# The opening of a two-stage graph network kernel, put in another order on all five engines

## The reference, cut to what matters

```python
h = jnp.maximum(_layernorm(x), 0.0)
x = x + _L0_gnn_ref(h, adj, W, a)      # masked attention, only the 16 largest weights of a row are kept, elu
h = jnp.maximum(_layernorm(x), 0.0)
x = x + _L1_gnn_ref(h, adj, ...)       # three layers
# one layer of L1:
scores = leaky(x @ w_i + (x @ w_j).T + b), -inf outside of (adj or the diagonal)
h  = layernorm(x + softmax(scores) @ x) * g1 + beta1
ff = gelu(h @ W1 + b1) @ W2 + b2       # 256 -> 1024 -> 256
x  = layernorm(h + ff) * g2 + beta2
```

## Time and profile before

| | |
|---|---|
| median of three runs | 2843.44 us (2842.48 to 2846.93) |
| span of the profiled execution, first to last instruction | 2840.5 us |
| PE busy | 2719.1 us, 96% of the span |
| PE weight load busy | 2449.2 us, 86% |
| ACT busy | 2326.9 us, 82% |
| DVE busy | 2293.8 us, 81% |
| POOL busy | 2080.0 us, 73% |
| mean granted clock of PE | 0.979 |

### The profile page before, as it was taken

The page is one execution under the profiler, slowest core; times in us unless marked ns, Lnnn a source line. Parts: engine busy times, 40 slices in busy tenths (PEclk is TensorE's granted clock), DMA queues, the critical chain, the costliest instruction groups (busy, mean ns, idle before and its releaser), DMA issues.

```text
span 2840.5 us, 55392 instructions
## 1 busy us (share of the span) xinstructions
PE 2719.1 (96%) x17764; PEld 2449.2 (86%) x17764; DVE 2293.8 (81%) x7766; ACT 2326.9 (82%) x4806; POOL 2080.0 (73%) x2217
## 2 busy tenths in 40 slices
...
DMA packets 96322, 88.63 MB, mean 31 GB/s; under 512 B 9120, under 2 KB 94368, under 8 KB 96032
## 3 DMA queue, kind: packets, MB, share of 16 engines
...
## 4 chain that ended last, share of the span: by engine, by line
PE 80%; POOL 5%; issue 5%; DVE 4%; ACT 3%; DMA 2%; POOLq 0%; SPq 0%; ACTq 0%; DVEq 0%
PE ps_ff L3065 11%; PE ps_mm L3042 11%; PE ps_mm L3044 11%; PE ps_mm L3043 10%; PE ps_ff L3066 10%; PE ps_ff L3067 10%; PE ps_ag L3100 5%; PE ps_ht L3112 3%; PE ps L3164 2%; DMA out<-H 2%; POOL a_lo L506 2%; PE ps_s L3088 1%; PE ps_s L3078 1%; PE ps L3177 1%; PE ps L3178 1%
## 5 line engine op out<-in xcount | busy, mean ns | idle before, releaser
L3065 PE MATMUL ps_ff<-w_hi,a_hi 128*128 128x256 f32 x3072 | 892.0, 290 | 10.1 <-POOL a_lo L506 5.3
L506 POOL TENSOR_TENSOR a_lo<-A,a_hi 128x512 fp32r<-128x512 f32 x384 | 524.3, 1366 | 486.7 <-ACT a_hi L1077 486.4
L3066 PE MATMUL ps_ff<-w_lo,a_hi 128*128 128x256 f32 x3072 | 855.6, 279 | 0.0
L3067 PE MATMUL ps_ff<-w_hi,a_lo 128*128 128x256 f32 x3072 | 855.0, 278 | 0.0
L1069 ACT ACTIVATE A<-ps_mm,b_col 128x512 f32<-128x512 f32 x768 | 517.3, 685 | 251.7 <-PE ps_ff L3067 147.8
L3042 PE MATMUL ps_mm<-ht_hi,w_hi 128*128 128x512 f32 x1536 | 627.0, 408 | 3.7 <-DVE ht_lo L2327 2.8
L3065 PEld LDWEIGHTS ps_ff<-w_hi,a_hi 128*128 128x128 f32 x3072 | 578.2, 188 | 45.7 <-issue 11.7
L3044 PE MATMUL ps_mm<-ht_lo,w_hi 128*128 128x512 f32 x1536 | 606.5, 395 | 0.0
L3043 PE MATMUL ps_mm<-ht_hi,w_lo 128*128 128x512 f32 x1536 | 604.6, 394 | 0.0
L3066 PEld LDWEIGHTS ps_ff<-w_lo,a_hi 128*128 128x128 f32 x3072 | 579.0, 188 | 12.5
L3067 PEld LDWEIGHTS ps_ff<-w_hi,a_lo 128*128 128x128 f32 x3072 | 579.2, 189 | 0.0
...
## 6 DMA issues: line engine op xcount, KB each, us to landing
...
X<-in_L_gnn_W SPq DMA_DIRECT2D x3, 1024.0 KB, 5.2
H<-in_L_gnn_W SPq DMA_DIRECT2D x3, 1024.0 KB, 7.1
```

Of the source, the lines that this page charges most:

```text
L506: pool.tensor_tensor(a_lo[:, at], A[:, at], a_hi[:, at].bitcast(F32), ALU.subtract).then_inc(s["a_lo_gpsimd"], 1)
L3065: pe.matmul(out_g, a_hi[:, at, cols], w2_hi[:, l, m], start=first, stop=False, skip_group_check=True)
L3066: pe.matmul(out_g, a_hi[:, at, cols], w2_lo[:, l, m], start=False, stop=False, skip_group_check=True)
L3067: last = pe.matmul(out_g, a_lo[:, at, cols], w2_hi[:, l, m], start=False, stop=final, skip_group_check=True)
```

## The change

All five opening() lists keep the same calls, in another order. iteration(i), closing() and every function that the lists call are as before. SP, ACT, DVE and PE have 56, 347, 309 and 330 calls, POOL 245.

In the new lists the loads of x(0), a0, W0 and of two adjacencies come ahead of W1(0) and W2(0). DVE begins with x_moments(0), ACT with x0_norm(0). The splits of the weights and bias_cols, bias_rows, w1_bias stand at other places: w1_low(1) ahead of z_max(1) and scores_mask(0,0), w1_low(2) ahead of y1_sum(1,0,0), w2_low(1) among the a_low of (0,0), w2_low(2) among those of (1,0), w1_bias(2) behind z_mix(1,0). masks(1), masks(2) and masks(3) stand earlier. From the first mm1 on, the order of attention, stage 0 and products changes at many places. The diff, cut; the lists go on in this manner:

```diff
@@ -328,61 +328,61 @@
 sp.dma_start(mask_in[:, l].rearrange("p g m -> p (g m)"), mask_park[value(k)]).then_inc(s_mask[l], 16)
 
 def opening():
-load_w0()
-load_w1(0)
 load_x(0)
 load_a0()
+load_w0()
+load_adj(0)
+load_adj(1)
 load_cols()
+park_mask(0)
+load_w1(0)
+load_w2(0)
+load_adj(2)
+load_wij()
 load_x(1)
-load_adj(0)
-load_w2(0)
+load_w1(1)
+load_mask(0, 0)
+store_x1(0)
+load_w2(1)
 load_rows()
-load_adj(1)
-load_wij()
-load_w1(1)
-park_mask(0)
-load_w2(1)
+park_mask(1)
+load_x(2)
 load_w1(2)
-load_w2(2)
-park_mask(1)
-load_mask(0, 0)
-load_adj(2)
-load_x(2)
-store_x1(0)
-park_mask(2)
-load_mask(1, 0)
-load_mask(0, 1)
-store_x1(1)
 load_x(3)
 load_adj(3)
...
@@ -544,170 +544,173 @@
 r_coefs(0)
 h_coefs(0, 0)
 h_scale(0, 0, 0)
+x_coefs(2)
+a_low(0, 0, 0)
 h_scale(0, 0, 1)
-h_bias(0, 0, 0)
-a_low(0, 0, 0)
-h_bias(0, 0, 1)
-x_coefs(2)
 a_low(0, 0, 2)
 r_coefs(1)
 a_low(0, 0, 4)
+h_bias(0, 0, 0)
+h_bias(0, 0, 1)
 a_low(0, 0, 6)
 y_coefs(0, 0)
 y_scale(0, 0, 0)
+y_bias(0, 0, 0)
 y_scale(0, 0, 1)
-y_bias(0, 0, 0)
 y_bias(0, 0, 1)
 h_coefs(1, 0)
+h_scale(1, 0, 0)
+x_coefs(3)
+a_low(1, 0, 0)
+h_scale(1, 0, 1)
 h_coefs(0, 1)
-h_scale(1, 0, 0)
+a_low(1, 0, 2)
 h_bias(1, 0, 0)
-h_scale(1, 0, 1)
-a_low(1, 0, 0)
+r_coefs(2)
+a_low(1, 0, 4)
+h_scale(0, 1, 0)
 h_bias(1, 0, 1)
-a_low(1, 0, 2)
-r_coefs(2)
-h_scale(0, 1, 0)
-a_low(1, 0, 4)
-x_coefs(3)
+h_bias(0, 1, 0)
+h_scale(0, 1, 1)
+h_bias(0, 1, 1)
 a_low(1, 0, 6)
-h_scale(0, 1, 1)
 a_low(0, 1, 0)
-h_bias(0, 1, 0)
 y_coefs(1, 0)
 a_low(0, 1, 2)
+x_coefs(4)
 y_scale(1, 0, 0)
 y_scale(1, 0, 1)
+h_coefs(2, 0)
 y_bias(1, 0, 0)
 y_bias(1, 0, 1)
 a_low(0, 1, 4)
 a_low(0, 1, 6)
-h_bias(0, 1, 1)
-h_coefs(2, 0)
...
@@ -1204,352 +1204,352 @@
 act.activation(flat(el[:]), flat(x1[:, two]), ACT.Exp).then_inc(s["elu_exped"], 1)
 
 def opening():
+x0_norm(0)
+wa_copy()
 w0_high()
-w1_high(0)
-wa_copy()
-w2_high(0)
-x0_norm(0)
 z_leaky(0)
 z_exps(0)
-w1_high(1)
-w2_high(1)
+w2_high(0)
+w1_high(0)
 z_copy(0)
 mix_high(0, 0)
 elu_exp(0, 0)
 mix_high(0, 1)
+w1_high(1)
 elu_exp(0, 1)
 x0_norm(1)
-w2_high(2)
 r_norm(0)
-w1_high(2)
+z_leaky(1)
 leaky(0, 0)
+z_exps(1)
 exps(0, 0)
 p_copy(0, 0)
-z_leaky(1)
-z_exps(1)
+w2_high(1)
+z_copy(1)
+mix_high(1, 0)
 h_norm(0, 0)
-z_copy(1)
 ht_high(0, 0, 0)
-mix_high(1, 0)
+mix_high(1, 1)
+elu_exp(1, 0)
 ht_high(0, 0, 1)
+x0_norm(2)
 gelu(0, 0, 0)
-mix_high(1, 1)
+gelu(0, 0, 1)
 a_high(0, 0, 0)
-gelu(0, 0, 1)
 a_high(0, 0, 1)
+elu_exp(1, 1)
 gelu(0, 0, 2)
-elu_exp(1, 0)
 a_high(0, 0, 2)
-elu_exp(1, 1)
 gelu(0, 0, 3)
+z_leaky(2)
+gelu(0, 0, 4)
 a_high(0, 0, 3)
-gelu(0, 0, 4)
 a_high(0, 0, 4)
+r_norm(1)
 gelu(0, 0, 5)
+w1_high(2)
 a_high(0, 0, 5)
-r_norm(1)
 gelu(0, 0, 6)
 a_high(0, 0, 6)
 gelu(0, 0, 7)
 a_high(0, 0, 7)
 leaky(1, 0)
-x0_norm(2)
+exps(1, 0)
+z_exps(2)
+p_copy(1, 0)
 y_norm(0, 0)
-exps(1, 0)
-p_copy(1, 0)
-z_leaky(2)
+w2_high(2)
+z_copy(2)
+mix_high(2, 0)
+h_norm(1, 0)
 leaky(0, 1)
-z_exps(2)
+ht_high(1, 0, 0)
 exps(0, 1)
+ht_high(1, 0, 1)
+mix_high(2, 1)
 p_copy(0, 1)
-h_norm(1, 0)
...
+a_high(1, 1, 2)
+ht_high(0, 2, 0)
+z_leaky(4)
+gelu(1, 1, 3)
+y_norm(2, 0)
+ht_high(0, 2, 1)
+a_high(1, 1, 3)
 leaky(3, 0)
-gelu(1, 1, 0)
-a_high(1, 1, 0)
-gelu(1, 1, 1)
-a_high(1, 1, 1)
+gelu(1, 1, 4)
+a_high(1, 1, 4)
 exps(3, 0)
-gelu(1, 1, 2)
+gelu(1, 1, 5)
+gelu(1, 1, 6)
 p_copy(3, 0)
-gelu(1, 1, 3)
-a_high(1, 1, 2)
-a_high(1, 1, 3)
-y_norm(2, 0)
-h_norm(0, 2)
-z_leaky(4)
-gelu(1, 1, 4)
-ht_high(0, 2, 0)
-a_high(1, 1, 4)
-gelu(1, 1, 5)
 a_high(1, 1, 5)
-ht_high(0, 2, 1)
-gelu(1, 1, 6)
+z_exps(4)
+a_high(1, 1, 6)
 gelu(1, 1, 7)
-a_high(1, 1, 6)
+gelu(0, 2, 0)
 a_high(1, 1, 7)
 leaky(2, 1)
-gelu(0, 2, 0)
-z_exps(4)
 a_high(0, 2, 0)
+gelu(0, 2, 1)
 exps(2, 1)
-gelu(0, 2, 1)
+z_copy(4)
 a_high(0, 2, 1)
 gelu(0, 2, 2)
+mix_high(4, 0)
 a_high(0, 2, 2)
 p_copy(2, 1)
+h_norm(3, 0)
 y_norm(1, 1)
+ht_high(3, 0, 0)
 gelu(0, 2, 3)
+gelu(0, 2, 4)
 a_high(0, 2, 3)
-gelu(0, 2, 4)
 a_high(0, 2, 4)
+elu_exp(4, 0)
 gelu(0, 2, 5)
-z_copy(4)
+mix_high(4, 1)
+gelu(0, 2, 6)
 a_high(0, 2, 5)
-h_norm(3, 0)
-ht_high(3, 0, 0)
-mix_high(4, 0)
-gelu(0, 2, 6)
 a_high(0, 2, 6)
-leaky(1, 2)
+ht_high(3, 0, 1)
+h_norm(2, 1)
 gelu(0, 2, 7)
 a_high(0, 2, 7)
-ht_high(3, 0, 1)
-h_norm(2, 1)
+elu_exp(4, 1)
+ht_high(2, 1, 0)
+leaky(1, 2)
+gelu(3, 0, 0)
...
@@ -2354,315 +2354,315 @@
 moments("y", n, lambda g: H[:, l, g])
 
 def opening():
+x_moments(0)
 wa_sums()
-x_moments(0)
 masks(0)
+e0_scores(0)
 w0_low()
-w1_low(0)
-e0_scores(0)
-w2_low(0)
 z_mask(0)
 z_max(0)
+masks(1)
 z_topk(0)
-bias_cols(0)
 z_recip(0)
-w2_low(1)
+w1_low(0)
 mix_low(0, 0)
-w1_low(1)
+x_moments(1)
 z_out(0, 0)
+w2_low(0)
+mix_low(0, 1)
 elu(0, 0)
-mix_low(0, 1)
-x_moments(1)
-masks(1)
 z_out(0, 1)
 elu(0, 1)
 r_moments(0)
+e0_scores(1)
 node_scores(0, 0)
+z_mask(1)
+w1_low(1)
+z_max(1)
 scores_mask(0, 0)
 scores_max(0, 0)
-e0_scores(1)
-w1_low(2)
+z_topk(1)
 recip(0, 0)
+z_recip(1)
+bias_cols(0)
+bias_rows()
 y1_sum(0, 0, 0)
-z_mask(1)
-z_max(1)
+masks(2)
 y1_sum(0, 0, 1)
 y1_moments(0, 0)
-z_topk(1)
+mix_low(1, 0)
+x_moments(2)
+z_out(1, 0)
+ht_low(0, 0, 0)
 bias_cols(1)
-w2_low(2)
-ht_low(0, 0, 0)
+mix_low(1, 1)
+ht_low(0, 0, 1)
+elu(1, 0)
+z_out(1, 1)
 bias_cols(2)
-mix_low(1, 0)
-bias_rows()
-ht_low(0, 0, 1)
-z_recip(1)
-z_out(1, 0)
-masks(2)
-mix_low(1, 1)
-x_moments(2)
-z_out(1, 1)
+e0_scores(2)
 a_low(0, 0, 1)
-elu(1, 0)
 elu(1, 1)
 r_moments(1)
+w2_low(1)
 a_low(0, 0, 3)
+z_mask(2)
+z_max(2)
+node_scores(1, 0)
 a_low(0, 0, 5)
-node_scores(1, 0)
+masks(3)
 a_low(0, 0, 7)
 scores_mask(1, 0)
+scores_max(1, 0)
 y_sum(0, 0)
+recip(1, 0)
 y_moments(0, 0)
-e0_scores(2)
-scores_max(1, 0)
-recip(1, 0)
+w1_low(2)
+y1_sum(1, 0, 0)
+z_topk(2)
+y1_sum(1, 0, 1)
+y1_moments(1, 0)
 node_scores(0, 1)
-z_mask(2)
-y1_sum(1, 0, 0)
-z_max(2)
+mix_low(2, 0)
 scores_mask(0, 1)
 scores_max(0, 1)
-y1_sum(1, 0, 1)
-y1_moments(1, 0)
...
@@ -3182,335 +3182,335 @@
 
 def opening():
 turn_wa()
+turn_e0(0)
 w1_bias(0)
-turn_e0(0)
-w1_bias(1)
 turn_z(0)
 z_mix(0, 0)
 z_agg(0, 0)
 z_mix(0, 1)
 z_agg(0, 1)
-w1_bias(2)
+w1_bias(1)
+turn_e0(1)
 turn_sj(0, 0)
 turn_p(0, 0)
-turn_e0(1)
 agg(0, 0, 0)
+turn_z(1)
 agg(0, 0, 1)
-turn_z(1)
+z_mix(1, 0)
+w1_bias(2)
+z_agg(1, 0)
 turn_h(0, 0, 0)
-z_mix(1, 0)
+z_mix(1, 1)
 turn_h(0, 0, 1)
-z_agg(1, 0)
+z_agg(1, 1)
 mm1(0, 0, 0)
-z_mix(1, 1)
 mm1(0, 0, 1)
 mm1(0, 0, 2)
-z_agg(1, 1)
 mm1(0, 0, 3)
 mm2(0, 0, 0)
+turn_e0(2)
 mm2(0, 0, 1)
 mm1(0, 0, 4)
 mm1(0, 0, 5)
 mm2(0, 0, 2)
+mm1(0, 0, 6)
 mm2(0, 0, 3)
-mm1(0, 0, 6)
+mm2(0, 0, 4)
 mm1(0, 0, 7)
-mm2(0, 0, 4)
+turn_sj(1, 0)
 mm2(0, 0, 5)
-turn_sj(1, 0)
 mm2(0, 0, 6)
 mm2(0, 0, 7)
-turn_e0(2)
 turn_p(1, 0)
 agg(1, 0, 0)
+agg(1, 0, 1)
+turn_z(2)
+z_mix(2, 0)
 turn_sj(0, 1)
-agg(1, 0, 1)
+turn_h(1, 0, 0)
+z_agg(2, 0)
+turn_h(1, 0, 1)
+z_mix(2, 1)
 turn_p(0, 1)
+mm1(1, 0, 0)
 agg(0, 1, 0)
-turn_z(2)
+mm1(1, 0, 1)
...
 mm1(0, 1, 5)
-mm2(0, 1, 2)
-turn_e0(3)
 mm2(0, 1, 3)
-agg(2, 0, 0)
 mm1(0, 1, 6)
 mm1(0, 1, 7)
+turn_h(2, 0, 0)
+turn_z(3)
 mm2(0, 1, 4)
+z_mix(3, 0)
+turn_sj(1, 1)
 mm2(0, 1, 5)
-turn_sj(1, 1)
-agg(2, 0, 1)
+turn_h(2, 0, 1)
 mm2(0, 1, 6)
 mm2(0, 1, 7)
+mm1(2, 0, 0)
 turn_p(1, 1)
+z_agg(3, 0)
 agg(1, 1, 0)
-turn_z(3)
+mm1(2, 0, 1)
+mm1(2, 0, 2)
 agg(1, 1, 1)
-turn_h(2, 0, 0)
-z_mix(3, 0)
-turn_sj(0, 2)
-turn_h(2, 0, 1)
-z_agg(3, 0)
-mm1(2, 0, 0)
 z_mix(3, 1)
-mm1(2, 0, 1)
-turn_p(0, 2)
-turn_h(1, 1, 0)
-mm1(2, 0, 2)
-z_agg(3, 1)
 mm2(2, 0, 0)
-turn_h(1, 1, 1)
 mm1(2, 0, 3)
 mm1(2, 0, 4)
 mm2(2, 0, 1)
 mm1(2, 0, 5)
+turn_sj(0, 2)
+z_agg(3, 1)
...
```

More of the change, by code:

```diff
@@ L2501, in opening @@
                 a_low(2, 0, 7)
-                scores_mask(3, 0)
-                scores_max(3, 0)
+                e0_scores(4)
                 y_sum(2, 0)
@@ L2619, in opening @@
                 a_low(4, 0, 7)
-                scores_mask(5, 0)
-                scores_max(5, 0)
+                recip(5, 0)
                 y_sum(4, 0)
                 y_moments(4, 0)
-                recip(5, 0)
+                ht_low(2, 2, 0)
+                z_mask(6)
+                y1_sum(5, 0, 0)
                 a_low(3, 1, 1)
-                e0_scores(6)
+                z_max(6)
+                x_moments(7)
+                y1_sum(5, 0, 1)
+                masks(7)
                 a_low(3, 1, 3)
-                y1_sum(5, 0, 0)
@@ L3314, in opening @@
                 mm1(1, 1, 3)
+                turn_h(0, 2, 0)
+                turn_e0(4)
                 mm2(1, 1, 0)
-                turn_p(3, 0)
+                mm1(1, 1, 4)
+                turn_h(0, 2, 1)
                 mm2(1, 1, 1)
-                mm1(1, 1, 4)
+                turn_sj(3, 0)
                 mm1(1, 1, 5)
                 mm2(1, 1, 2)
-                turn_e0(4)
-                agg(3, 0, 0)
-                turn_h(0, 2, 0)
                 mm2(1, 1, 3)
                 mm1(1, 1, 6)
-                turn_h(0, 2, 1)
+                mm2(1, 1, 4)
@@ L3327, in opening @@
+                turn_p(3, 0)
                 mm1(1, 1, 7)
-                agg(3, 0, 1)
-                mm2(1, 1, 4)
+                agg(3, 0, 0)
```

(41 more changed lines are left out.)

859 lines of the change are left out of this document (422 added, 437 removed).

## The result

The changed kernel takes 2883.5 us (median of four runs, 2880.1 to 2885.4); the kernel before, beside it, 2844.0 (2842.5 to 2846.9). The ratio is 1.0138, with a 95% interval from 1.0124 to 1.0152: it is slower by 39 us, where 2821 was forecast.

A forecast was written before the change was run, and what follows sets the result against it. TensorE bounds the kernel, working 2719.1 of 2840.5 us, so mainly its 121.4 us idle can be won. Lead 28.5 less 6 for table loads is 22.5, rounded to 22: 2840.5 - 22 + 2.9 = 2821 us, range 2806 to 2841.

The forecast's parts named there:

- The moments of the beginning: Starts forecast: turn_z(0) 25.5, mm1(0,0,0) 84.5, turn_p(1,0) 113.5, mm1(1,0,0) 138.1, mm1(2,0,0) 198.0 us.
- the net lead of 28.5: Lead of 31.7 us at mm1(2,0,0), less about 3.2 of earlier work still owed.
- Two sums of the prediction: turn_z(0): W1(0) issue 13.5, landing 5.2, w1_bias 6.98, giving 25.5; turn_p(1,0): mask/max 1.6, load 1.28, exps 1.7, giving 3.1.
- third moment: First mm1 of group 1, mm1(1,0,0): forecast at 138.1 us, a lead of 15.1.
- about 4.1: Time in us taken for z_topk(2), newly placed ahead of y1_sum(1,0,1), between turn_p(1,0) and mm1(1,0,0).
- The block of group 1: Stretch from mm1(1,0,0) to mm1(2,0,0): 52.6 + 2.3 + 5 = 59.9 us, with the hole behind it gone.
- the stall of 5: In group 1's block, nearly full VectorE is late: 0 at best, 11 if half the hole stays, 5 us taken.
- From 242 us on TensorE is full: In the kernel before, TensorE is busy 236.7 of 238 us from 242 us on.
- the 6 us of table loads: Behind mm1(2,0,0): 12 more ScalarE table loads, six round trips, cost TensorE 6 us, between 0 and 23.
- TensorE idles over 10 us between 200 and 480: Sign in the profile after, times in us, that would show the forecast wrong.
- rival (c): Table trips on the path, exponentials between gelus whose mm1 banks TensorE awaits, clock lowered: 2850 us, chance 0.10.
- e0_scores: VectorE step; before, e0_scores(2) stood ahead of scores_max(1,0), in the hole where turn_p(1,0) came 10.5 us after the block.

The follow-up runs named there:

- bn_after: Changed kernel, groups 1 to 8, with node_scores' reductions made bn_stats and z_topk's last step made max: 2845.9 us; same edit in the order before 2841.1.
- c240: Changed order for calls started by 240 us, then the order of the kernel before: 2836.5 us, ratio to before 0.9974.
- r240: Order of the kernel before for calls started by 240 us, then the changed order: 2900.1 us, ratio to before 1.0194.
- short_after: Changed kernel with GpSimd's h_scale, h_bias, y_scale, y_bias on 32 of 256 columns in groups 1 to 8: 2839.3 us; same edit in order before 2843.7.

## Why the prediction was wrong

**The moments of the beginning: right.** The five were off by 2.0, -3.4, -2.9, -1.2 and 4.6 us, and the net lead of 28.5 was 24.4 at 240. turn_z(0) came right behind w1_bias(0), as said, but W1(0) landed at 20.7 instead of 18.7. mm1(0,0,0) was early, near the 80 that I had given for the full clock, and the full clock came at about 69 us instead of 92: four products of 128 columns took 1.06 us at 67.01, eight took 1.05 at 69.69. (The 1.00 that the row gives for the whole of 54.70 to 92.27 is too high for its first part, by these times.) Two sums of the prediction do not close, and neither decides: 13.5 + 5.2 + 6.98 is 25.7, not 25.5, and 1.6 + 1.28 + 1.7 is 4.6, where I wrote that turn_p(1,0) comes 3.1 behind the block; it came 1.6 behind it.

**Inside the third moment a term was wrong and hidden.** I gave z_topk(2) "about 4.1". It took 8.3 (115.53 to 123.8), its last step being the 5.30 shown above. The moment still came 1.2 us early, since turn_p(1,0) was early by 2.9 and the rest of that stretch was shorter than I had it.

**The block of group 1: the same fault, under another name.** "VectorE has some 51 us of work in it ... I take 5". The stretch took 65.63 us, not 59.9, with VectorE busy 58.96: the stall of 5 was 10.7. I had added the operations at their lone durations, so the clashes were missing from the sum. Without those of two of them (bn_after) the lead at 200 us is 17.3, not 7.8.

**The step that failed: "From 242 us on TensorE is full", and the 6 us of table loads as all that is "added behind that".** I read from the earlier trace rows that TensorE is full there and let the moved lists of groups 3 to 6 pass at no cost, 6 us of tables apart. It was full only as long as its feeders kept up, and VectorE had 42 us of slack in 238 (195.78 busy). In the new order the same operations stand beside GpSimd's long steps, VectorE gets 1022 instead of 1158 instructions done in 400 us, and 62 us of lead go: c240 and r240 place that behind 240 us. What the pairs of runs show of the cause is this. Of the 39.5 us by which the kernel is slower, 34.7 go with the clashes of two operations. Of the 62 behind 240 us, 26 go with them, and 43 when GpSimd's long steps are short; the rest, 35 us in the one run and 19 in the other, is not shown to be clashes, and most of it stays open (below). "TensorE idles over 10 us between 200 and 480", a sign that I gave for being wrong, is what happened: from 242 to 480 us it is busy for 215.71 of 238.

**Table loads.** The count was right (12 more), the cost of 6 was not there: without any, the two orders stand 41.6 us apart. The Trainium skill's 2.66 us a switch ("ScalarE: Activation LUTs", section "What ACT_TABLE_LOAD costs"), which I had set aside, would have given a slower kernel, but not by the cause that was at work. The rows stay with 1.30: in the earlier trace rows the loads of L1131, L1204 and L1186 have 0.1 us of idle time ahead of all of a group together, and in the earlier trace rows the activation follows at once. The rival (c), "exponentials stand between two gelus whose mm1 banks TensorE waits for", named 2850, and falls with it: right in sign, wrong in mechanism.

**What I could have seen.** The trace of before has the clash in it: the two L2172 groups of VectorE above are one form, the reductions of e0_scores, and take 582 and 416 ns. The difference is three instructions of 1.51 us (at 435.93, 519.70 and 603.10), and each has an a_low of GpSimd beside it.

**What stays open.** Even without these clashes the changed order does not keep its lead: 36.3 at 240, 15.9 at 500, 0.8 at 620 in bn_after. One piece of that is the order's own. The last a_low of GpSimd's opening list, a_low(5,1,0), stands behind y_coefs(6,0) and y_bias(3,2,0) in the changed list and ahead of them in the list before. TensorE and GpSimd of bn_after there:

```profile
597.30 0.55 PE L3072 MATMUL ps_ff<-w_hi,a_hi 128*128 128x256 f32 x1 [5.91 <-POOL a_lo L507]
```

```profile
592.03 0.56 POOL L445 TENSOR_TENSOR st_y_ve<-st_y_mv,eps_col 128x4 f32<-128x4 f32 x1 [0.73 <-DVE st_y_mv L2117]
...
594.32 1.44 POOL L524 TENSOR_TENSOR H<-H,be_row 128x512 f32<-128x512 f32 x1
595.72 1.44 POOL L507 TENSOR_TENSOR a_lo<-A,a_hi 128x512 fp32r<-128x512 f32 x1
```

y_coefs waits for VectorE's moments, a_low stands behind y_coefs and y_bias although ScalarE's a_high was done by 591.5, and TensorE waits 5.91 us for a_low. The same wait is 5.55 us in short_after and 7.80 in r240 and in the changed kernel, and before has no wait of over 0.3 us from 560 to 700 us: it does not go with the clashes. The other waits on a_lo are a further part, and elu, masks and e0_scores still clash; which share of the rest is theirs, which is work that was put off, and which is the order's own was not tried. Nor was there a run of an order that keeps the new groups 3 to 6 and moves only GpSimd's long steps away from VectorE's, or of one that moves a_low(5,1,0) alone.
